# All attention matmuls on tiles of 64 rows by 32 columns, v's products by row halves into two banks

## The chip, the cores and the metric

The kernel runs on one core of one Trainium2 chip. The metric is device time in microseconds. The kernel before takes 1523.57 us, the median of three runs (1523.52 to 1525.18).

Engines by the names of the profile: PE is TensorE's matmul stream and PEld its weight loads, DVE is VectorE, ACT is ScalarE, POOL is GpSimd, SP is SyncE, which issues nearly all DMAs.

## The reference

A macaron transformer block on x of shape (2, 2048, 256), float32:

```
x = x + 0.5 * ffn(layernorm(x))
x = x + attention(layernorm(x))        # 16 heads of 16, softmax over 2048 keys, then @ wo.T + bo
x = x + 0.5 * ffn(layernorm(x))        # the same weights
ffn(h):  h = [h, -h] @ k0 (512 x 1024, entries +-1), * s0, relu, * 2
         h = h @ k1 (1024 x 1024), * s1, relu, * 2
         h = h @ k2 (1024 x 256), * s2
```

For each batch and head, scores are q k^T / 4, a softmax over the keys, and the product with v.

## The kernel before

**Blocks and layers.** The 4096 tokens go in 8 blocks of 512. For each block the feed-forward is three layers: l1 (8 output tiles of 128, inner dimension 256), l2 (8 tiles, inner 1024) and l3 (back to 256, tokens on partitions, 256 columns a matmul). Activations are held as two fp16 terms, a high and a low one, so each product is computed twice, with h_hi and with h_lo. A tile of l1 or l2 is emptied from PSUM in two operations: relu into the high term (ACT, L915, or DVE, L980), then relu minus the high term into the low one (DVE, L982). For q and k it is the same with L922 or L996, then L998. l3 is emptied by L987, v by L1006, the output projection by L1013, all on DVE.

**Attention.** A group is four heads of one block of 512 queries: 2 batches x 4 query blocks x 4 = 32 groups. The 2048 keys are 16 tiles of 128. An attention step (`Step("att", n)`) takes two key tiles of one group, so there are 8 steps a group and 256 in all. A step has 8 score banks of 128 keys by 512 queries: `pe_scores` (L856 to L874) computes them in four pairs of heads. Each matmul takes 64 rows (the four products of high and low terms of q and k, 16 dimensions each), so the two heads of a pair run on the upper and the lower 64 rows of the array, with 128 columns each. ACT takes the exponential of a bank, or of two neighbouring ones, into `prob` (`act_exps`, L942). `pe_values` (L876) multiplies the exponentials of the step before with v and a column of ones: 8 matmuls in fp32, 128 rows by 17 columns, the four heads of a key tile at partitions 0, 32, 64 and 96 of one bank (`O_BANK`). An fp32 matmul shows as two records. After 16 key tiles `dve_o` copies the bank out (L1115) and SP stores it. The division by the sum of the exponentials comes later (L1106, L1108).

**What is interleaved.** From attention's first step on, the other blocks' layers are cut into slots that are laid between the scores of the steps. `lay_pair` takes two banks of a layer at a time, always banks 6 and 7 (`SHARED`). In `pe_pair` (L798 to L854) one slot is two matmuls of 64 rows, one for each bank, on different row halves; after half of the slots the two banks change row halves, and PE waits for `halves` there (L816). At its first slot a pair waits until ACT and DVE have emptied both banks of the pair before (L802 to L806). The list `PAIRS` says how many slots a step holds and how they are divided by the scores; a step holds 8 slots of l1 or l2, 16 of l3, 2 of q and k, 4 of v or of the output projection. A pair of l1 banks has 8 slots (one step), of l2 32 (four steps), of l3 64 (four steps), of q and k 4, of v or the output 8 (two steps each). In a pair, the first bank of l1, l2, q and k is emptied wholly by DVE, the second by ACT (high) and DVE (low).

**Order.** The list `work`, written before the program, fixes the order on every engine; each engine walks it and takes its own parts, in order. A step of before is: scores of pairs 0 and 1; slots; score 2; slots; score 3; the values of the step before, both key tiles. Scores rotate over five banks (`SCORES`, 0 to 4), and a score waits (L864) for the exponential that read its bank last. Long DVE work (norms, splits, divisions) is laid behind a step's first scores (`lay_long`). In four steps the sum of squares of q and k (L775, 128 rows by 32 columns) takes one of the score banks (`lay_column`).

Before and after attention the layers are computed with matmuls of 128 rows by 128 columns (`pe_fill`, L738 for l1, L750 for l2, L762 for l3) in a ring of banks `WHOLE`, which is the score banks and the shared ones.

## Time and profile before

| | |
|---|---|
| runs | 1523.57 us median, 1523.52 to 1525.18 |
| profiled execution, span from first to last instruction | 1521.2 us |
| PE, PEld | 1512.4 us (99%), 606.1 us (40%) |
| ACT | 1129.3 us (74%) |
| DVE | 574.2 us (38%) |
| granted TensorE clock, mean | 0.999 |

The profile has no time of its own for the profiled execution beside its span; the span lies 2.4 us under the median of the runs.

A row of the time line has the start (us), the length (us, from the first start to the last end of the merged instructions), engine, line, operation, the tiles written and read, the shape and the count. A matmul's row lasts longer than the array is taken by it, since its filling and draining are in it: two matmuls that start 0.216 us apart each last 0.38. Times between starts are therefore what is to be read. In a matmul's shape `64*128` are the rows and columns of the array that its weights take, and `64x512` the moving data.

### The profile page before, as it was taken

Reading aid. Unit: us, or ns where it says so; the run is one execution under the profiler, and the core shown is the slowest. Engines: PE = TensorE matmul, PEld = TensorE weight load, DVE = VectorE, ACT = ScalarE, POOL = GpSimd, SP = SyncE. Lnnn points to the kernel's source line nnn. Section 1 sums busy time; section 2 is a strip of 40 time slices with the busy share of each in tenths; the row PEclk is TensorE's granted clock in tenths of the full one; section 3 lists DMA queues with packets and bytes.
Section 4 is the critical chain, followed back from the end, with each engine's and each line's share of the span. In section 5 each row is a group of like instructions: output and inputs, shape, how many; then the busy total and the mean of one; then the engine's idle time right before and its main releaser. Section 6 shows DMA issues by size and latency. Waiting matters only on the chain.

```text
span 1521.2 us, 31574 instructions
## 1 busy us (share of the span) xinstructions
PE 1512.4 (99%) x12471; PEld 606.1 (40%) x12471; DVE 574.2 (38%) x1298; ACT 1129.3 (74%) x1654; POOL 59.7 (4%) x65
## 2 busy tenths in 40 slices
PE   9999999999999999999999999999999999999999
PEld 5555455334334333333333334334333334334354
DVE  7645764511431243234332333242241332323462
ACT  3221222888889988898989989889988988988721
POOL 2010011001000100010100000000000000000000
PEclk9999999999999999999999999999999999999999
DMA  4122223212331231232223123111213212311110
GB/s 139 42 84 51 75 80 113 71 51 81 84 73 41 96 95 40 67 113 63 81 53 95 40 53 94 39 49 59 81 39 67 82 51 65 104 41 21 47 28 16
DMA packets 110139, 101.46 MB, mean 67 GB/s; under 512 B 55846, under 2 KB 95526, under 8 KB 109990
## 3 DMA queue, kind: packets, MB, share of 16 engines
q1 hardware_dynamic: 109158, 98.60, 23.0%
q8 instruction: 105, 1.72, 0.5%
q10 hardware_dynamic: 832, 0.79, 0.2%
q14 instruction: 44, 0.36, 0.1%
HBM read 61.87 MB, written 25.43 MB: 57 GB/s over the span
## 4 chain that ended last, share of the span: by engine, by line
PE 99%; DVE 0%; ACT 0%; issue 0%; POOL 0%; POOLq 0%
PE psum L888 31%; PE psum L850 30%; PE psum L872 16%; PE psum L750 12%; PE psum L762 3%; PE psum L738 3%; PE psum L769 2%; PE psum L782 1%; PE psum L688 0%; PE psum L775 0%; DVE xn L972 0%; DVE h_lo L982 0%; PE psum L710 0%; DVE x_sb L987 0%; ACT xn L911 0%
## 5 line engine op out<-in xcount | busy, mean ns | idle before, releaser
L942 ACT ACTIVATE prob<-psum 128x512 f32<-128x512 f32 (+1 forms) x1438 | 1016.6, 784 | 120.1 <-PE psum L872 115.4
L888 PE MATMUL psum<-prob,v_sb 128*17 128x512 f32 x4096 | 489.4, 595 | 0.0
L872 PE MATMUL psum<-q_st,k_st 64*128 64x512 f16 x2048 | 350.1, 379 | 0.2
L915 ACT ACTIVATE h_hi<-psum 128x512 f16<-128x512 f32 x183 | 109.6, 604 | 215.8 <-PE psum L750 164.6
L980 DVE TENSOR_SCALAR h_hi<-psum 128x512 f16<-128x512 f32 x73 | 50.5, 692 | 433.8 <-PE psum L850 433.8
L982 DVE SCALAR_TENSOR_TENSOR h_lo<-psum,h_hi 128x512 f16<-128x512 f32 x256 | 169.0, 688 | 86.9 <-ACT h_hi L915 84.4
L888 PEld LDWEIGHTS psum<-prob,v_sb 128*17 128x17 f32 x4096 | 95.3, 96 | 262.9 <-issue 166.4
L872 PEld LDWEIGHTS psum<-q_st,k_st 64*128 64x128 f16 x2048 | 82.5, 94 | 279.1 <-ACT prob L942 210.7
L850 PE MATMUL psum<-h_hi,w 64*128 64x512 f16 x1184 | 152.1, 376 | 0.2 <-ACT h_hi L915 0.2
L850 PE MATMUL psum<-h_lo,w 64*128 64x512 f16 x1184 | 152.0, 376 | 0.0
L750 PE MATMUL psum<-h_hi,w 128*128 128x512 f16 x432 | 102.5, 380 | 2.2 <-DVE h_lo L982 2.2
L750 PE MATMUL psum<-h_lo,w 128*128 128x512 f16 x432 | 103.4, 383 | 0.0
L850 PEld LDWEIGHTS psum<-h_hi,w 64*128 64x128 f16 x1184 | 58.0, 94 | 70.3 <-DVE h_lo L982 1.7
L850 PEld LDWEIGHTS psum<-h_lo,w 64*128 64x128 f16 x1184 | 57.8, 94 | 69.8
L1115 DVE COPY o_sb<-psum 128x512 f32<-128x512 f32 x32 | 22.1, 692 | 165.2 <-PE psum L888 164.8
L850 PE MATMUL psum<-xn,w 64*128 64x512 f16 x576 | 74.3, 377 | 0.0
L987 DVE SCALAR_TENSOR_TENSOR x_sb<-psum,scal,x_sb 128x512 f32<-128x512 f32 x32 | 23.2, 748 | 108.4 <-PE psum L850 77.4
L750 PEld LDWEIGHTS psum<-h_lo,w 128*128 128x128 f16 x432 | 42.7, 99 | 52.5 <-issue 2.2
L750 PEld LDWEIGHTS psum<-h_hi,w 128*128 128x128 f16 x432 | 42.2, 98 | 53.1 <-issue 2.7
L1106 DVE RECIPROCAL den_t<-den_t 128x128 f32<-128x128 f32 x64 | 60.5, 945 | 3.3 <-DMA den_t<-den_rows 3.3
L738 PE MATMUL psum<-xn,w 128*128 128x512 f16 x224 | 50.4, 379 | 1.1 <-ACT xn L911 0.9
L850 PE MATMUL psum<-w,h_lo 64*128 64x256 f16 x576 | 43.2, 269 | 0.0
(109 smaller groups left out, 860.0 us busy)
## 6 DMA issues: line engine op xcount, KB each, us to landing
k_st<-k_halves SPq DMA_DIRECT2D x64, 512.0 KB, 4.4
q_halves<-piece SPq DMA_DIRECT2D x32, 256.0 KB, 2.5
q_st<-q_halves SPq DMA_DIRECT2D x64, 128.0 KB, 4.8
x_rows<-x_sb SPq DMA_DIRECT2D x16, 256.0 KB, 2.2
k_halves<-piece SPq DMA_DIRECT2D x16, 256.0 KB, 2.8
att_rows<-o_sb SPq DMA_DIRECT2D x128, 32.0 KB
x_sb<-x_rows SPq DMA_DIRECT2D x8, 512.0 KB, 4.0
att_t<-att_rows SPq DMA_DIRECT2D x16, 256.0 KB
```

The lines of the kernel that those rows point to most:

```text
L738: mm = pe.matmul(psum[:, bank, :], w0[:, k, m * P:(m + 1) * P], xt[:, half, k, :], start=(j == 0), stop=(j == s.n - 1))
L750: mm = pe.matmul(psum[:, bank, :], w1[:, k, m * P:(m + 1) * P], (h0_hi, h0_lo)[half][:, k, :], start=(j == 0), stop=(j == s.n - 1))
L762: mm = pe.matmul(psum[:, bank, t * dim:(t + 1) * dim], (h1_hi, h1_lo)[half][:, k, tile * P:(tile + 1) * P], w2[:, k, :], start=(jj == 0), ...
L769: mm = pe.matmul(psum[:, bank, :], w[:, j, half * P:(half + 1) * P], at[:, j, :], start=(j == 0), stop=(j == kd - 1))
L850: mm = pe.matmul(to, w, a, start=(turned == 0 and j == 0), stop=(turned == 1 and j == length - 1))
L872: mm = pe.matmul(psum[:, score_bank[h + r], :], k_st[rows, slot, t * P:(t + 1) * P], q_st[rows, slot, :], start=True, stop=True)
L888: mm = pe.matmul(psum[32 * j:32 * j + va, O_BANK, :], v_sb[:, b * key_tiles + t, GROUP * g4 + j, :], prob[:, h % PROBS, :], start=(t == 0) ...
L915: act.activation(hi, psum[:, bank, :], ACT.Relu).then_inc(act_done, 1)
L942: act.activation(prob[:, to:to + count, :], psum[:, bank:bank + count, :], ACT.Exp, scale=score_scale / QK_SCALE ** 2).then_inc(exp_sem, 1)
L980: dve.tensor_scalar(hi[:, m, :], psum[:, bank, :], 0.0, None, ALU.max).then_inc(dve_done, 1)
L982: dve.scalar_tensor_tensor(lo[:, m, :], psum[:, bank, :], 0.0, hi[:, m, :], ALU.max, ALU.subtract).then_inc(dve_done, 1)
L1106: dve.reciprocal(den_t[:, half, cols], den_t[:, half, cols]).then_inc(den_inv, 1)
```

## The change

- Scores and all interleaved layers: each matmul of 64 rows by 128 columns becomes four of 64 rows by 32 columns (`QUARTERS`), each writing 32 partitions of the same bank.
- `pe_values`: each matmul of 128 rows by 17 columns becomes two of 64 rows by 17 columns, the upper keys into bank 4, the lower into bank 5 (`O_BANKS`). It is called once for each key tile, the two calls at different places in the step.
- `dve_o`: a copy of the one bank and then an addition of the other, with a wait between them.
- Four score banks instead of five; all exponentials are of two banks, but for one pair in a step with a column. A column takes two places in the rotation of the banks (`score_skip`).
- `WHOLE` has six banks instead of seven.
- The order of a step: score 0; slots; score 1; slots; the values of the first key tile of the step before; score 2; slots; score 3; the values of the second key tile. The slots of a step are as many as before, in three parts instead of two; for l1 and l2 2, 2 and 4.

```diff
@@ -121,8 +121,8 @@
-    SCORES = [0, 1, 2, 3, 4]
-    O_BANK = 5
+    SCORES = [0, 1, 2, 3]
+    O_BANKS = [4, 5]
     SHARED = [6, 7]
     def projections(u):
@@ -204,7 +204,7 @@
     ahead_of_attention = [s.kind in FILLS for s in side[:[(s.kind, s.u) for s in side].index(("l2", qblocks + 1))]]
-    in_turn = SCORES[:4] + SHARED + SCORES[4:]
+    in_turn = SCORES + SHARED
     WHOLE = [in_turn[(i - sum(ahead_of_attention)) % len(in_turn)] for i in range(len(in_turn))]
     numbers = Numbers()
@@ -227,7 +227,7 @@
-    PAIRS = {"l1": (4, 4), "l2": (5, 3), "l3": (10, 6), "qk": (1, 1), "v": (2, 2), "out": (2, 2)}
+    PAIRS = {"l1": (2, 2, 4), "l2": (2, 2, 4), "l3": (4, 4, 8), "qk": (0, 1, 1), "v": (1, 1, 2), "out": (1, 1, 2)}
     LONG = {"norm": 1.0, "xn": 0.3, "split": 0.4, "flip": 1.0, "merge": 0.4, "heads": 0.26, "peak": 0.3}
@@ -300,6 +300,10 @@
                 exp_groups.append((h, count))
                 exp_done.extend(count * (len(exp_groups),))
+    def score_skip():
+        taken.append(taken[-len(SCORES)])
     def lay_column(s):
         kind, h = taken[-len(SCORES)]
         assert kind == "exp"
@@ -307,6 +311,7 @@
         lay(s, SCORES[len(taken) % len(SCORES):][:1], False)
         taken.append(("dve", s.dve - 4 if s.kind == "range" else s.dve))
+        score_skip()
     for n in range(att_steps):
         work.append(Step("att", n))
@@ -318,25 +323,28 @@
         elif n >= 4 and side[0].hi + sum(PAIRS["l2"]) < 2 * FILLS["l2"][0]:
             lay_long(1.0)
-        for between, slots in enumerate(((5, 3), (3, 3), (3, 2), (3, 2))[n] if n < 4 else PAIRS[side[0].kind]):
-            lay_pair(slots)
+        for between, slots in enumerate(((2, 2, 4), (2, 2, 2), (1, 2, 2), (1, 2, 2))[n] if n < 4 else PAIRS[side[0].kind]):
+            if slots:
+                lay_pair(slots)
+            if between == 1 and n:
+                work.append(Step("values", n - 1, 0))
             work.append(Step("score", n, 1 + between))
         if n == 0:
             lay_pair(8)
         if columns and not side[0].n:
-            lay_exps(n, ((0, 1), (1, 2), (3, 1), (4, 1), (5, 2), (7, 1)))
+            lay_exps(n, ((0, 2), (2, 2), (4, 1), (5, 1), (6, 2)))
             lay_column(columns.pop(0))
         else:
-            lay_exps(n, ((0, 1), (1, 2), (3, 2), (5, 2), (7, 1)))
+            lay_exps(n, ((0, 2), (2, 2), (4, 2), (6, 2)))
         if n:
-            work.append(Step("values", n - 1))
+            work.append(Step("values", n - 1, 1))
             if n % group_steps == 0:
                 work.append(Step("o", n // group_steps - 1))
         if n == group_steps * (groups // 2 - 1):
             assert ("v", blocks - 1, 1) in find
-    work.append(Step("values", att_steps - 1))
+    work += [Step("values", att_steps - 1, tile) for tile in range(2)]
     work.append(Step("o", groups - 1))
     while held:
@@ -520,7 +528,7 @@
             sem(n) for n in ("ln", "ln_x", "split", "flipped", "merged", "squared", "peaked", "bo_added", "halves"))
         qk_sem, exp_sem, pv_sem = sem("qk"), sem("exp"), sem("pv")
-        o_copied, den_inv, att_ready = sem("o_copied"), sem("den_inv"), sem("att_ready")
+        o_half, o_copied, den_inv, att_ready = sem("o_half"), sem("o_copied"), sem("den_inv"), sem("att_ready")
         g_zero, g_in, g_pe, g_max, g_mout, g_mrow, g_exp, g_pv, g_o = (
             sem(n) for n in ("g_zero", "g_in", "g_pe", "g_max", "g_mout", "g_mrow", "g_exp", "g_pv", "g_o"))
@@ -666,10 +674,9 @@
                 if s.kind == "att":
                     pe_attention(s.u)
                 elif s.kind == "score":
-                    for pair in ((0, 1), (2,), (3,))[s.m]:
-                        pe_scores(s.u, pair)
+                    pe_scores(s.u, s.m)
                 elif s.kind == "values":
-                    pe_values(s.u)
+                    pe_values(s.u, s.m)
                 elif s.kind == "att_end":
                     pe.wait_ge(exp_sem, len(exp_groups))
@@ -795,6 +802,8 @@
             return 2 * tpb * out_no(u) + tpb + per_bank * (m + 1)
+        QUARTERS = [slice(c, c + P // 4) for c in range(0, P, P // 4)]
         def pe_pair(s):
             u, n = s.u, s.mate.n
@@ -835,7 +844,7 @@
                 for bank, first in ((s, 0), (s.mate, 1)):
                     r, m = (first + turned + part) % 2, bank.m
                     rows, cols = slice(64 * r, 64 * r + 64), slice(m * P, (m + 1) * P)
-                    to = psum[:, bank.bank, :]
+                    wide = slice(0, BANK)
                     if s.kind == "l1":
                         w, a = w0[rows, k, cols], xt[rows, term, k, :]
                     elif s.kind == "l2":
@@ -845,9 +854,11 @@
                     else:
                         tile = m * per_bank + column
                         src, wide_w = {"l3": ((h1_hi, h1_lo)[term], w2), "v": (at, wv_sb), "out": (att_t, wo_sb)}[s.kind]
-                        to = psum[:, bank.bank, column * dim:(column + 1) * dim]
+                        wide = slice(column * dim, (column + 1) * dim)
                         w, a = src[rows, k, tile * P:(tile + 1) * P], wide_w[rows, k, :]
-                    mm = pe.matmul(to, w, a, start=(turned == 0 and j == 0), stop=(turned == 1 and j == length - 1))
+                    for c in QUARTERS:
+                        mm = pe.matmul(psum[c, bank.bank, wide], w[:, c], a,
+                                       start=(turned == 0 and j == 0), stop=(turned == 1 and j == length - 1))
                     if i == 2 * n - 1:
                         mm.then_inc(mm_done, 1)
                     elif not turned and j == length - 1:
@@ -869,25 +880,28 @@
                     pe.wait_ge(dve_done, left[1])
             for r in range(2):
                 rows = slice(64 * r, 64 * r + 64)
-                mm = pe.matmul(psum[:, score_bank[h + r], :], k_st[rows, slot, t * P:(t + 1) * P], q_st[rows, slot, :],
-                               start=True, stop=True)
+                for c in QUARTERS:
+                    mm = pe.matmul(psum[c, score_bank[h + r], :], k_st[rows, slot, t * P:(t + 1) * P][:, c],
+                                   q_st[rows, slot, :], start=True, stop=True)
             mm.then_inc(qk_sem, 1)
-        def pe_values(n):
+        def pe_values(n, tile):
             g, tp = divmod(n, group_steps)
             b, g4 = g // (qblocks * block_groups), g % block_groups
-            for tile in range(2):
-                t = 2 * tp + tile
-                if t == 0:
-                    pe.wait_ge(o_copied, O_ZEROED + g)
-                    pe.wait_ge(dve_done, find["v", (b + 1) * qblocks - 1, 1].dve)
-                for j in range(GROUP):
-                    h = STEP_BANKS * n + GROUP * tile + j
-                    if j % 2 == 0:
-                        pe.wait_ge(exp_sem, exp_done[h + 1])
-                    mm = pe.matmul(psum[32 * j:32 * j + va, O_BANK, :], v_sb[:, b * key_tiles + t, GROUP * g4 + j, :],
-                                   prob[:, h % PROBS, :], start=(t == 0), stop=(t == key_tiles - 1))
-                mm.then_inc(pv_sem, 1)
+            t = 2 * tp + tile
+            if t == 0:
+                pe.wait_ge(o_copied, O_ZEROED + g)
+                pe.wait_ge(dve_done, find["v", (b + 1) * qblocks - 1, 1].dve)
+            for j in range(GROUP):
+                h = STEP_BANKS * n + GROUP * tile + j
+                if j % 2 == 0:
+                    pe.wait_ge(exp_sem, exp_done[h + 1])
+                for r in range(2):
+                    rows = slice(64 * r, 64 * r + 64)
+                    mm = pe.matmul(psum[32 * j:32 * j + va, O_BANKS[r], :],
+                                   v_sb[rows, b * key_tiles + t, GROUP * g4 + j, :], prob[rows, h % PROBS, :],
+                                   start=(t == 0), stop=(t == key_tiles - 1))
+            mm.then_inc(pv_sem, 1)
         def pe_attention(n):
             if n % group_steps == 0:
@@ -900,7 +914,7 @@
             for s in steps:
                 u, m, bank = s.u, s.m, s.bank
                 if s.kind == "score":
-                    act_exps(s.u, (0, 4, 6)[s.m], (4, 6, 8)[s.m])
+                    act_exps(s.u, 2 * s.m, 2 * s.m + 2)
                 elif s.kind == "w1":
                     act_w1()
                 elif not s.on_act or s.kind not in FILLS or not s.last():
@@ -1112,7 +1126,9 @@
             dve.wait_ge(pv_sem, key_tiles * (g + 1))
             if g >= 2:
                 dve.wait_ge(o_out[g % 2], O_MOVE * (g // 2))
-            dve.tensor_copy(o_sb[:, g % 2, :], psum[:, O_BANK, :]).then_inc(o_copied, 1)
+            dve.tensor_copy(o_sb[:, g % 2, :], psum[:, O_BANKS[0], :]).then_inc(o_half, 1)
+            dve.wait_ge(o_half, g + 1)
+            dve.tensor_tensor(o_sb[:, g % 2, :], psum[:, O_BANKS[1], :], o_sb[:, g % 2, :], ALU.add).then_inc(o_copied, 1)
         def dve_peak():
             dve.wait_ge(dve_done, find["sq", blocks - 1, 0].dve)
@@ -1376,7 +1392,7 @@
         sp_loads()
         act_loads()
         dve.memset(table[:], 1.0).then_inc(table_seed, 1)
-        dve.memset(psum[:, O_BANK, :], 0.0).then_inc(o_copied, 1)
+        dve.memset(psum[:, O_BANKS[0]:O_BANKS[1] + 1, :], 0.0).then_inc(o_copied, 1)
         act.wait_ge(table_seed, 1)
         act.activation(table[0:1, 0:1], table[0:1, 1:2], ACT.Exp).then_inc(table_ready, 1)
         act_factors()
```

## Rows read from the trace of the kernel before

**Rows 1.** Busy time of the engines, from the page.

```profile
PE 1512.4 (99%) x12471; PEld 606.1 (40%) x12471; DVE 574.2 (38%) x1298; ACT 1129.3 (74%) x1654; POOL 59.7 (4%) x65
```

**Rows 2.** The chain that ended last, shares by engine, from the page.

```profile
PE 99%; DVE 0%; ACT 0%; issue 0%; POOL 0%; POOLq 0%
```

**Rows 3.** Attention: length, then PE, PEld, DVE, ACT, POOL busy; clock, DMA share, GB/s.

```profile
278.18:1431.06 1152.88, 1152.70 (x10579) 415.15 (x10575) 370.10 (x781) 1033.85 (x1503) 35.15 (x24) 1.00 0.23 66
```

**Rows 4.** Time line of PE over one l2 step.

```profile
857.60 0.60 PE L872 MATMUL psum<-q_st,k_st 64*128 64x512 f16 x4
858.04 1.24 PE L850 MATMUL psum<-h_lo,w 64*128 64x512 f16 x10
...
859.99 0.38 PE L872 MATMUL psum<-q_st,k_st 64*128 64x512 f16 x2
860.30 1.91 PE L888 MATMUL psum<-prob,v_sb 128*17 128x512 f32 x16
862.14 0.60 PE L872 MATMUL psum<-q_st,k_st 64*128 64x512 f16 x4
```

**Rows 5.** Time lines of PE and DVE where a pair of q and k ends.

```profile
365.21 0.38 PE L872 MATMUL psum<-q_st,k_st 64*128 64x512 f16 x2
365.43 0.59 PE L850 MATMUL psum<-at,wk_sb 64*128 64x512 f32 x1
...
365.86 0.59 PE L850 MATMUL psum<-at,wk_sb 64*128 64x512 f32 x1
...
368.00 0.74 DVE L998 SCALAR_TENSOR_TENSOR piece<-psum,bk_sb,piece 128x512 f16<-128x512 f32 x1
```

**Rows 6.** Time line of PE in an l1 step, where the row halves change.

```profile
1409.48 0.38 PE L872 MATMUL psum<-q_st,k_st 64*128 64x512 f16 x2
1409.73 0.39 PE L850 MATMUL psum<-xn,w 64*128 64x512 f16 x2
```

**Rows 7.** Time lines of PE and DVE where a pair of l3 ends.

```profile
356.80 0.60 PE L850 MATMUL psum<-w,h_lo 64*128 64x256 f16 x8
...
357.43 1.41 DVE L987 SCALAR_TENSOR_TENSOR x_sb<-psum,scal,x_sb 128x512 f32<-128x512 f32 x2 [10.89 <-PE psum L850]
```

**Rows 8.** Time lines of DVE, PE and PEld where DVE was late.

```profile
286.30 0.69 DVE L982 SCALAR_TENSOR_TENSOR h_lo<-psum,h_hi 128x512 f16<-128x512 f32 x1 [0.42 <-ACT h_hi L915]
...
287.14 0.61 PE L850 MATMUL psum<-h_hi,w 64*128 64x512 f16 x4
...
287.11 0.14 PEld L850 LDWEIGHTS psum<-h_hi,w 64*128 64x128 f16 x4
```

**Rows 9.** A group by line and shape: count, busy us, mean ns, idle before.

```profile
L775 PEld LDWEIGHTS psum<-square,head_ones 128*32 128x32 bf16 x16 | 0.8, 92 | 3.4 <-issue 2.1 <-ACT h_hi L915 1.3
```

**Rows 10.** Time line of ACT, one narrow and two wide exponentials.

```profile
1408.60 2.43 ACT L942 ACTIVATE prob<-psum 128x512 f32<-128x512 f32 x3 [0.60 <-PE psum L872]
```

**Rows 11.** Time lines of PE and DVE where an l2 pair ends.

```profile
850.27 0.81 PE L850 MATMUL psum<-h_lo,w 64*128 64x512 f16 x6
...
853.51 0.59 PE L850 MATMUL psum<-h_hi,w 64*128 64x512 f16 x4
...
851.12 0.69 DVE L980 TENSOR_SCALAR h_hi<-psum 128x512 f16<-128x512 f32 x1 [16.07 <-PE psum L850]
851.84 1.29 DVE L982 SCALAR_TENSOR_TENSOR h_lo<-psum,h_hi 128x512 f16<-128x512 f32 x2
```

**Rows 12.** Line 982 in attention (count, ns min/median/max); time lines, output pair's end.

```profile
L982 DVE SCALAR_TENSOR_TENSOR h_lo<-psum,h_hi x144: 678/691/693, 285.2 to 1425.9; 128x512 f16<-128x512 f32 x144
...
776.98 0.81 PE L850 MATMUL psum<-wo_sb,att_t 64*128 64x256 f32 x6
777.90 1.29 DVE L1013 TENSOR_TENSOR x_sb<-psum,x_sb 128x512 f32<-128x512 f32 x2 [7.13 <-PE psum L850]
```

**Rows 13.** Time lines of PE and DVE where a group ends.

```profile
856.63 1.04 PE L888 MATMUL psum<-prob,v_sb 128*17 128x512 f32 x8
...
857.74 0.69 DVE L1115 COPY o_sb<-psum 128x512 f32<-128x512 f32 x1 [1.05 <-PE psum L888]
```

## The prediction

> **What bounds the kernel now.** I read the busy shares first: TensorE (PE) is busy for 99% of the span, ScalarE (ACT) for 74%, VectorE (DVE) for 38% [rows 1]. The chain that ended last says it in another way: 99% of it is PE [rows 2]. So what the change does to PE's order and waits is what it does to the time. The attention steps fill 278.18 to 1431.06 us, 253 whole steps and 76% of the span, with the granted clock at 1.00 (2.4 GHz) [rows 3]: 4.557 us a step.
>
> A PE row counts as busy from its start to a modelled end, so "99%" hides lost time; I find it from the starts. In one step [rows 4] scores start at 857.60, fills at 858.04, the last score at 859.99, v's products at 860.30 and the next scores at 862.14: 4.54 us. From 858.04 to 859.99 there are eight fill slots and a score, nine waves: a wave of 512 fp16 columns takes 0.216 us. Slots of q and k, in fp32, follow each other at 365.43 and 365.86 [rows 5]: a pass of 512 fp32 columns takes 0.43 us. A step holds 4 score waves, 8 fill waves and 4 passes: 12 x 0.216 + 4 x 0.43 = 4.31 us. The other 0.225 us lies where the tile shape changes: from the last score to the first product is 0.31 (0.09 too much), from the products to the next scores 1.84 instead of 1.72 (0.12); 0.01 is left. Between fills and scores, both 64x128, nothing is lost.
>
> **The change, part by part.**
>
> *One tile shape (64 rows by 32 columns).* The waves keep their number if the eight tiles run together: scores and fills 8 matmuls a wave instead of 2, v's products 8 on two row halves and four column groups, still 4 passes a step. Both changes of shape vanish. Of 256 steps I take off the two at the ends: gain 254 x 0.225 = 57.2 us; the bounds are 0 (the loss belongs to something else) and these 57. The four square steps keep their 128-row matmuls and so two changes: 0.9 us back. The wait between a pair's halves makes a wave of 0.25 us in an l1 step instead of 0.216, with the load behind it 0.05 in all [rows 6]; now products and scores lie there. With 36 l1 steps in attention (nine blocks of four pairs, a pair a step) that gives 1.8 us.
>
> *More instructions.* An l2 step has 128 matmuls and 128 loads instead of 40 and 40; an l3 step 192 and 192. The densest stream is that of l3: four slots (eight matmuls) last 0.60 us [rows 7], so with the slot of 0.109 us (four instructions) it is 27 ns each, and there the array was the limit, not the feed. The near end is a release from a wait: in program order loads and matmuls alternate, so the fourth load is the seventh instruction, and it starts 0.14 - 0.09 = 0.05 us after the first, 8 ns each [rows 8]. Needed are 16 per 216 ns (13 ns) in l2 and 16 per 109 ns (7 ns) in l3. At the far end an l2 step takes 256 x 0.027 = 6.9 us for 4.31, in all some +700 us. I take the near end, at no cost: it is the row with the array free. A load of 32 columns takes 92 ns [rows 9], less than the shortest slot, so loads hide.
>
> *Exponentials in pairs.* The eight banks of a step go as four wide ACT instructions. One narrow and two wide in a row take 2.43 us, so a wide one costs (2.43 - 0.61) / 2 = 0.91 [rows 10]. Four are 3.64, with a fill's relu 4.24 us: under 4.31, so ACT stays behind PE. I take 0; late by the relu once per l2 pair would be 36 x 0.5 = 18.
>
> *The place of the fills: a new wait.* This decides. DVE and ACT must empty a pair's banks (6 and 7) before the next pair may start. In an l2 pair of before the last slot starts at 850.27 + 2 x 0.216 = 850.70 and the next pair at 853.51, 2.81 later [rows 11]. DVE's three evacuations begin at 851.12 and end at 851.84 + 1.29 = 853.13 (the same group), 2.43 after the last slot. How long from there to PE's matmul shows where DVE was late: end 286.30 + 0.69 = 286.99, matmul 287.14, so 0.15 [rows 8]. Release is at 2.58, with 0.23 of slack today.
> The new order after the last slot is score, products of one key tile only (2 passes), score, fill: 0.216 + 0.216 + 0.86 + 0.216 = 1.51 us. So PE waits 2.58 - 1.51 = 1.07 us, with the second score (and its exponential) and the other products queued behind. By kind, with the pairs counted in the order of work (nine blocks' l1, l2 and l3, four blocks' q, k and v, seven blocks' output):
> - l1 and l2: 72 pairs (as the 144 h_lo say [rows 12]) x 1.07 = 77.0
> - l3: last slot 357.13, DVE ends 358.84 [rows 7], release at 1.86; order 0.109 + 1.292 = 1.40; 9 x 0.46 = 4.1
> - q and k: last slot 365.86, DVE ends 368.74 [rows 5], release at 3.03; order 0.43 + 1.292 = 1.72, or 1.94 ahead of another such pair; 4 x 1.31 + 4 x 1.09 = 9.6
> - output, and v taken the same: last slot 777.41, DVE ends 779.19 [rows 12], 1.93 against 1.51; 11 x 0.42 = 4.6
>
> Together 95.3 us for 100 pairs. From below, 0.04 instead of 0.15 for the release gives 84; from above, a long norm on DVE ahead of an evacuation adds some us.
>
> *The output of a group.* Two banks mean a copy (0.69) and an add (0.69, the same operation as the output's two in 1.29 [rows 12]), the add 0.72 after the copy's start as in the first two of [rows 11]: 1.41 us. DVE starts 0.07 after the products' end, 857.67 to 857.74 [rows 13], so 1.57 after the last slot; it ends at 2.98 and frees PE at 3.13. The next group's first product stands at 1.292 + 0.216 + 0.432 + 0.216 + 0.432 = 2.59: 0.54 us of wait. Where the step ended a pair (100 of 254), DVE begins at about 2.35 and PE is itself late: 3.91 against 2.59 + 1.07, 0.25. Mean 0.43 x 31 = 13.3 us. Bounds 0 (hidden, as the copy is now) and 20.
>
> *Outside attention* a ring of six banks replaces seven; a bank of l1 lasts four waves, 0.86 us, and is emptied within 2.6, so six are enough: 0.
>
> **Sum**, on the profiled execution: -57.2 + 0.9 - 1.8 + 95.3 + 13.3 = +50.5, a span of 1571.7 instead of 1521.2 us. The median of the runs, 1523.57, is 2.4 above that span, so 1574.
>
> **Rivals.**
> (a) *The feed falls behind in l3.* If an instruction takes half of the 27 ns of [rows 7], 13.6, an l2 step just fits and an l3 step takes 384 x 0.0136 = 5.22 instead of 4.33 us: 36 x 0.89 = 32 us, 1606. For it: no row shows a denser stream for more than seven instructions. Against it: those seven. The Trainium skill, "TensorE: Matmul & The Clock Gate", section "Wait — 56ns, not 53.3ns?", says that starts never come closer than about 25 ns however small the matmul; by that an l3 slot of eight would take 0.2 instead of 0.109 us, and my estimate from its figure is 36 x 16 x 0.091 = 52 us more. For different tiles the trace disagrees, with seven instructions in 0.05 us.
> (b) *The eight tiles do not run together* (row halves and column groups at once stand in no row, each alone does). Every fp16 wave doubled is 254 x 12 x 0.216 = 658 us, about 2235.
> (c) *The loss between shapes stays*, since it belongs to the turn from fp16 to fp32: 1574 + 57 = 1631. Against it: fp32 q and k follow fp16 scores at the usual distance, 365.21 to 365.43 [rows 5].
> (d) *The other side: the fill wait does not bind.* Its place is the first load after a step's first score. If PE let the second score and the products pass the waiting load, or the release came early, the gain would stand. It decides from 57.2 + 1.8 - 0.9 - 13.3 = 45 us over 100 pairs: 0.45 each instead of 0.95, for l1 and l2 a release 2.0 us after the last slot instead of 2.58. With no fill wait the time is 1574 - 95 = 1479. Against it: DVE ends 2.43 after the slot, and all of PE's instructions stand in one order.
>
> **Chances.** Forecast 0.73 (own range 1554 to 1590), (a) 0.12, (b) 0.03, (c) 0.05, (d) 0.07. The range 1552 to 1612 takes in the forecast with its bounds and (a). Under 0.2% (3 us) a measurement can't tell from none: faster 0.07, same 0.02, slower 0.91.
>
> **What would show it.** Right: no gap above a wave between scores and products; an l2 step in which no pair starts near 4.31 us, an l1 step near 5.4; a new pair's first matmul 0.15 us after DVE's last evacuation; more ACT idle time, put down to scores. Wrong: fill waves above 0.22 or 0.11 us (a, b), still 0.3 us from score to product (c), a pair's first matmul 1.5 us after the last slot (d).

## The result, and the profile after

The kernel with the change takes 1677.45 us, median of 4 runs (1670.65 to 1681.11), against 1523.57: 1.0998 times as long, with an interval of 1.0982 to 1.1013. The forecast was 1574, its range ended at 1612. The direction was right and the size was not: +154 us instead of +50.

The page of the kernel after: span, busy time [rows 1], the queue that brings instructions, and the chain [rows 2].

```profile
span 1676.2 us, 78723 instructions
PE 1522.6 (91%) x36439; PEld 806.7 (48%) x36439; DVE 593.9 (35%) x1330; ACT 1140.3 (68%) x1245; POOL 59.7 (4%) x65
q8 instruction: 292, 4.78, 1.2%
PE 80%; DVE 10%; issue 8%; ACT 2%; DMA 0%; ACTq 0%; DVEq 0%
```

PE has fallen from 99% to 91%, and the chain that was PE alone now holds DVE (the wait for a pair's banks, forecast) and 8% "issue", time in which PE waited for nothing that the profile shows. The instruction queue q8 brought 292 pages of 16 KB; before it had been:

```profile
q8 instruction: 105, 1.72, 0.5%
```

What ended PE's idle time in the kernel after (us in total, times, longest):

```profile
PE psum L860 <- DVE h_lo L996: 59.5, 64, 1.3
PE psum L860 <- issue: 41.9, 38, 4.4
PE psum L901 <- issue: 13.0, 12, 3.3
PE psum L884 <- issue: 10.8, 10, 2.4
```

Where nothing disturbs it, the new step is what the prediction made of it. PE's time line of the kernel after over one l2 step, which answers to [rows 4]:

```profile
869.81 0.43 PE L884 MATMUL psum<-q_st,k_st 64*32 64x512 f16 x8
870.02 0.64 PE L860 MATMUL psum<-h_lo,w 64*32 64x512 f16 x16
...
873.04 0.43 PE L884 MATMUL psum<-q_st,k_st 64*32 64x512 f16 x8
873.26 1.07 PE L901 MATMUL psum<-prob,v_sb 64*17 64x512 f32 x16
874.12 0.43 PE L884 MATMUL psum<-q_st,k_st 64*32 64x512 f16 x8
```

A wave of eight matmuls takes 0.216 us, score to products is a wave (873.04 to 873.26) and no longer 0.31, and the step from 869.81 to 874.12 takes 4.31 us. So the eight tiles do run together. At 521.02 it goes otherwise, in an l3 step:

```profile
521.02 0.78 PE L860 MATMUL psum<-w,h_lo 64*32 64x256 f16 x36
526.18 1.04 PE L860 MATMUL psum<-w,h_lo 64*32 64x256 f16 x28 [4.38 <-issue]
526.80 0.84 PE L884 MATMUL psum<-q_st,k_st 64*32 64x512 f16 x8
527.23 2.12 PE L901 MATMUL psum<-prob,v_sb 64*17 64x512 f32 x16
```

PE stops in the middle of a run of matmuls of one kind, between two that nobody else's work separates, for 4.38 us, and the waves behind it take 0.43 us instead of 0.216 until 530. The windows of the kernel after show why these waves are slow (length, PE, PEld, DVE, ACT, POOL busy, clock, DMA share, GB/s): the granted clock fell from 1.00 (2.4 GHz) to 0.50 (1.2 GHz) during the stall and stayed there when PE was busy again.

```profile
516.00:520.80 4.80, 4.41 (x200) 3.06 (x186) 0.00 (x0) 4.02 (x4) 0.00 (x0) 1.00 0.44 107
521.60:525.80 4.20, 0.20 (x14) 0.00 (x0) 0.00 (x0) 0.79 (x1) 0.00 (x0) 0.76 0.58 181
523.90:530.50 6.60, 4.32 (x100) 2.91 (x107) 0.99 (x2) 1.67 (x2) 0.00 (x0) 0.50 0.04 13
```

By kind of step, worked out from the trace as distances between the attention steps (255 of them, each from the start of the last matmul of a step's first pair of scores to that of the next step; sums in us). The last row is the experiment e10, explained below:

| | l2 (145) | l3 (36) | q, k (16) | v (8) | l1 (36) | output (14) | all |
|---|---|---|---|---|---|---|---|
| before | 657.3 | 164.1 | 72.9 | 36.8 | 166.8 | 64.1 | 1162.0 |
| after | 702.8 | 224.2 | 78.6 | 43.6 | 198.2 | 72.5 | 1319.9 |
| after, median step | 4.34 | 5.75 | 4.67 | 5.72 | 5.42 | 5.45 | |
| the tenth experiment | 667.1 | 170.7 | 79.9 | 39.4 | 188.4 | 71.2 | 1216.7 |

The sum grows by 158 us and the span by 155; outside attention 3 us were gained. The largest part is l3, the densest in instructions: 384 of PE a step, against 256 in l2.

### The profile page after: what moved, and what is told of

It reads as the page before. It is cut to its first block, busy times and chain, and to the rows that moved or that the text cites. A ratio compares the mean times of both kernels' runs of the same rounds, so it can differ in the third digit from the quotient of the medians.

```text
span 1676.2 us, 78723 instructions
## 1 busy us (share of the span) xinstructions
PE 1522.6 (91%) x36439; PEld 806.7 (48%) x36439; DVE 593.9 (35%) x1330; ACT 1140.3 (68%) x1245; POOL 59.7 (4%) x65
## 4 chain that ended last, share of the span: by engine, by line
PE 80%; DVE 10%; issue 8%; ACT 2%; DMA 0%; ACTq 0%; DVEq 0%
PE psum L860 27%; PE psum L901 22%; PE psum L757 11%; PE psum L884 11%; DVE h_lo L996 4%; PE psum L769 3%; DVE h_hi L994 3%; PE psum L745 3%; PE psum L776 2%; ACT prob L956 1%; PE psum L789 1%; DVE o_sb L1129 1%; DVE o_sb L1131 1%; DVE x_sb L1001 1%; DVE v_sb L1020 0%
## 5 line engine op out<-in xcount | busy, mean ns | idle before, releaser
L956 ACT ACTIVATE prob<-psum 128x1024 f32<-128x1024 f32 x1029 | 1024.0, 1020 | 265.8 <-PE psum L884 248.7
L901 PE MATMUL psum<-prob,v_sb 64*17 64x512 f32 x8192 | 590.8, 593 | 17.2 <-issue 13.0
L884 PE MATMUL psum<-q_st,k_st 64*32 64x512 f16 x8192 | 492.2, 379 | 18.3 <-issue 10.8
L884 PEld LDWEIGHTS psum<-q_st,k_st 64*32 64x32 f16 x8192 | 168.2, 92 | 220.0 <-ACT prob L956 114.6
L901 PEld LDWEIGHTS psum<-prob,v_sb 64*17 64x17 f32 x8192 | 159.2, 94 | 115.9 <-issue 45.6
L860 PE MATMUL psum<-h_hi,w 64*32 64x512 f16 x4736 | 182.8, 377 | 29.5 <-DVE h_lo L996 25.8
L996 DVE SCALAR_TENSOR_TENSOR h_lo<-psum,h_hi 128x512 f16<-128x512 f32 x256 | 168.1, 686 | 83.8 <-ACT h_hi L929 81.3
L860 PE MATMUL psum<-h_lo,w 64*32 64x512 f16 x4736 | 186.3, 379 | 7.7 <-issue 7.7
L860 PEld LDWEIGHTS psum<-h_hi,w 64*32 64x32 f16 x4736 | 85.3, 92 | 110.3 <-DVE h_lo L996 42.5
L860 PEld LDWEIGHTS psum<-h_lo,w 64*32 64x32 f16 x4736 | 91.4, 93 | 75.4 <-issue 44.5
L860 PE MATMUL psum<-xn,w 64*32 64x512 f16 x2304 | 87.6, 377 | 23.6 <-DVE h_lo L996 18.9
L860 PEld LDWEIGHTS psum<-xn,w 64*32 64x32 f16 x2304 | 36.8, 92 | 71.4 <-DVE h_lo L996 33.2
L757 PEld LDWEIGHTS psum<-h_hi,w 128*128 128x128 f16 x432 | 42.2, 98 | 51.2 <-issue 0.6
L757 PEld LDWEIGHTS psum<-h_lo,w 128*128 128x128 f16 x432 | 42.2, 98 | 51.0
```

The costliest lines, as they stand in the source:

```text
L757: mm = pe.matmul(psum[:, bank, :], w1[:, k, m * P:(m + 1) * P], (h0_hi, h0_lo)[half][:, k, :], start=(j == 0), stop=(j == s.n - 1))
L860: mm = pe.matmul(psum[c, bank.bank, wide], w[:, c], a, start=(turned == 0 and j == 0), stop=(turned == 1 and j == length - 1))
L884: mm = pe.matmul(psum[c, score_bank[h + r], :], k_st[rows, slot, t * P:(t + 1) * P][:, c], q_st[rows, slot, :], start=True, stop=True)
L901: mm = pe.matmul(psum[32 * j:32 * j + va, O_BANKS[r], :], v_sb[rows, b * key_tiles + t, GROUP * g4 + j, :], prob[rows, h % PROBS, :], star ...
L956: act.activation(prob[:, to:to + count, :], psum[:, bank:bank + count, :], ACT.Exp, scale=score_scale / QK_SCALE ** 2).then_inc(exp_sem, 1)
L996: dve.scalar_tensor_tensor(lo[:, m, :], psum[:, bank, :], 0.0, hi[:, m, :], ALU.max, ALU.subtract).then_inc(dve_done, 1)
```

## The experiments

Ratios are to the kernel before, with 95% intervals. The theory: PE's instructions come in pages of 256 (16 KB), and the pages come too slowly. Rivals: the order (the fill wait larger than forecast), the eight tiles themselves, or the four score banks.

**e1: the order of before, two tiles a wave.** The four banks and the halved products stay. Of the edit, the lists and the tiles are shown; the lines that lay both key tiles' products at the step's end and two score pairs at its start are left out here.

```
-    PAIRS = {"l1": (2, 2, 4), "l2": (2, 2, 4), "l3": (4, 4, 8), ...}
+    PAIRS = {"l1": (4, 4), "l2": (5, 3), "l3": (10, 6), ...}
-                    for c in QUARTERS:
+                    for c in [slice(0, P)]:
```

> v's products by row halves (64x17) into two banks and four score banks, but the order of before (both key tiles at the step's end, slots 5 and 3) and scores and fills on 64x128 tiles. It has 4096 matmuls more than before, not 23968. If the loss at the change of shape hangs on the rows alone (128 to 64), it is gone here and nothing else is added: a step of 4.31 us, about 1467 to 1475 us. If it hangs on the columns too (128 to 32), the 0.3 us from score to product stay: about 1523. The theory that instruction fetch makes the part of the loss that I had not forecast expects no page stall here, since a step has 96 instructions; the theory that eight tiles at once are slow expects the products to take more than 0.43 us a pass.

Measured 1576.3 us, 1.0342 [1.0325, 1.0359]. Both expected times were missed: the four score banks and the halved products in the old order cost 53 us by themselves. PE's time line over one l2 step:

```profile
869.02 0.61 PE L881 MATMUL psum<-q_st,k_st 64*128 64x512 f16 x4
869.46 1.24 PE L857 MATMUL psum<-h_lo,w 64*128 64x512 f16 x10
870.62 0.39 PE L881 MATMUL psum<-q_st,k_st 64*128 64x512 f16 x2
870.83 0.82 PE L857 MATMUL psum<-h_lo,w 64*128 64x512 f16 x6
871.53 0.39 PE L881 MATMUL psum<-q_st,k_st 64*128 64x512 f16 x2
871.86 1.94 PE L898 MATMUL psum<-prob,v_sb 64*17 64x512 f32 x32
873.73 0.61 PE L881 MATMUL psum<-q_st,k_st 64*128 64x512 f16 x4
```

The step takes 4.71 us, 0.40 above twelve waves and four passes. Score to products is 0.33 (0.11 too much) and products to scores 1.87 (0.15), although both now use 64 rows: 128 columns against 17 are enough for the loss between shapes. Five fill waves take 1.16 instead of 1.08 and three 0.70 instead of 0.65: both times the score behind them waits for the exponential that frees its bank.

**e2: the new order, two tiles a wave** (only the second edit of e1).

> The changed kernel with its order, but scores and fills on 64x128 tiles again (2 matmuls a wave, not 8): the instructions of the change are taken away, its waits are not. Fetch theory: no stall longer than the fill wait, and the time is that of e1 plus the forecast's two waits, 95 and 13 us: about 1575 if e1 is near 1467 (1630 if e1 is near 1523, and more since products now stand at two places of a step). Rival, the order alone makes all of the loss: within 1% of the changed kernel, 1677.

Measured 1671.51, 1.0965 [1.0947, 1.0984], with no idle time of PE put down to issue and 137 pages. The condition set for the rival (within 1% of the change) is met, yet the rival isn't shown by it, for this is another sum: an l2 step is 4.816 us (median), 0.51 above 4.307, with four changes of shape in it, and PE has none of the 65.7 us that it loses to issue in the change. The likeness of the totals is luck. Together e1 and the forecast's two waits would be 1685.

**e3: the old order, eight tiles** (only the first edit of e1).

> The changed kernel with all its 64x32 tiles, in the order of before: the waits are taken away, the instructions are not. Fetch theory: 1467 plus the 100 us that the forecast did not have, about 1570, with gaps of 1 to 4 us on PE that end about 1.3 us after a page of instructions has landed. Rival (the order alone): 1467 to 1480, with no such gaps.

Measured 1677.17, 1.1023 [1.1005, 1.1041]: the order of before doesn't save the eight tiles. Its waits:

```profile
PE psum L857 <- issue: 44.7, 37, 5.1
PE psum L881 <- issue: 29.9, 20, 4.5
PE psum L898 <- issue: 16.1, 17, 3.1
```

The fill wait is gone and the loss by issue has grown to 90.7 us; a median l2 step takes 4.496, an l3 step 6.24. The time is 107 us above the 1570 expected, mostly because that was built on 1467 for e1.

**e4: the new order, only the fills on 64 x 128.**

> The changed kernel with only the fills back on 64x128 tiles; scores stay on 64x32. An l2 step has 160 instructions instead of 256, an l3 step the same instead of 384. Fetch theory: the page stalls go, about the time of e2. If going between 64x128 and 64x32 costs what a change of shape cost before (0.1 us), six changes more in a step are 254 x 0.6 = 150 us more than e2.

Measured 1727.24, 1.1332 [1.1313, 1.1351]: the slowest. It is 56 us above e2, not 150: a step has six changes of shape against e2's four, not six more. They make the l2 step 5.02 us, 0.71 above 4.307. PE's time line in it:

```profile
850.14 0.40 PE L884 MATMUL psum<-q_st,k_st 64*32 64x512 f16 x8
850.47 0.61 PE L860 MATMUL psum<-h_hi,w 64*128 64x512 f16 x4
851.01 0.41 PE L884 MATMUL psum<-q_st,k_st 64*32 64x512 f16 x8
...
854.08 0.41 PE L884 MATMUL psum<-q_st,k_st 64*32 64x512 f16 x8
854.30 1.04 PE L901 MATMUL psum<-prob,v_sb 64*17 64x512 f32 x16
```

Score to fill takes 0.33 (0.12 too much), fill to score 0.54 for two waves of 0.43 (0.11); from 32 to 17 columns, 854.08 to 854.30, nothing is lost.

**e5: a probe.** Ahead of the kernel before, PE runs waves of matmuls on ready data with no waits. From 25.6 us on nothing else runs; the kernel's own loads, still under way, fall into the first stretch. One execution only, read by its trace.

```
+ for size, n, waves in ((32, 512, 64), (32, 256, 128), (32, 128, 96),
+                        (128, 256, 64), (128, 128, 128), (128, 64, 128)):
+   each wave: 2 row halves x 128/size column tiles, n columns moved
```

> The kernel before with a stretch of fp16 matmuls put in front of it, back to back with no waits: eight tiles of 64x32 with 512 columns (64 waves), 256 (128 waves), 128 (96 waves), then two tiles of 64x128 with 256, 128 and 64 columns. It measures the feed by itself. Fetch theory: 512 columns, 16 instructions a wave, a page of 256 in 16 waves of 0.216 = 3.5 us, just about sustained (0.216 to 0.24 us a wave); 256 columns is limited by pages, 0.22 to 0.24 us a wave instead of 0.109; 128 columns the same 0.22 to 0.24. In the two-tile stretches a wave of 4 instructions can't be below 0.055 to 0.06, so 256 and 128 columns take 0.109 and 0.06, and 64 columns 0.055 to 0.06 instead of 0.03. Rival (dispatch as fast as the 8 ns of the release row, pages no limit): 0.216, 0.128, 0.128 and 0.109, 0.055, 0.032.

The time line of PE in the second stretch, eight tiles with 256 columns (the first row begins in the stretch of 512 and runs into it):

```profile
25.19 3.82 PE L704 MATMUL psum<-ident 64*32 64x512 f16 x216
30.29 1.94 PE L704 MATMUL psum<-ident 64*32 64x256 f16 x128 [1.28 <-issue]
33.74 1.94 PE L704 MATMUL psum<-ident 64*32 64x256 f16 x128 [1.51 <-issue]
```

This is the cause by itself. PE runs exactly 128 matmuls and 128 loads, 256 instructions, and stops; the next 256 begin 3.45 us after the last 256 began. That is the shortest round: over the twelve rounds from 30.29 to 75.57 it is 3.45 to 4.00 us, 3.77 on average (14.7 ns an instruction). Set against the transfers of q8, a round has three parts: the next page's transfer starts 1.04 to 1.15 us after PE has begun a page, takes 0.9 to 1.5, and PE begins that page 1.35 to 1.59 us after its end. The rounds differ by the transfer's length. The DMA view of 25 to 42 us shows what comes meanwhile, 16 KB at a time, with all other queues silent (packets, MB, share):

```profile
DMA packets 4, 0.07 MB, mean 4 GB/s; under 512 B 0, under 2 KB 0, under 8 KB 0
q8 instruction: 4, 0.07, 1.6%
```

Within a page the stream is quick: 128 waves of eight took 28.52 us in all, but the median wave took 0.109, 16 instructions at 7 ns each. Two tiles of 128 columns run without a stop, and their 128 waves are 512 instructions in 7.07 us, 13.8 ns each, about the quickest rate of the pages. The first, second and fifth stretch in the window view:

```profile
5.35:25.60 20.25, 15.74 (x512) 7.85 (x519) 4.00 (x20) 0.00 (x0) 0.00 (x0) 0.93 0.63 186
25.64:54.16 28.52, 16.87 (x1032) 15.12 (x1024) 0.00 (x0) 0.00 (x0) 0.00 (x0) 0.92 0.02 5
...
85.53:92.60 7.07, 7.07 (x258) 7.07 (x254) 0.00 (x0) 0.00 (x0) 0.00 (x0) 1.00 0.02 5
```

Eight tiles with 256 and with 128 columns took 0.223 and 0.229 us a wave, as expected, the second at a clock of 0.50. Two tiles with 256 columns took 0.141, not 0.109, at a mean clock of 0.76. Two tiles with 64 columns took 0.045, below the expected 0.055 to 0.06: 512 instructions in 5.82 us is more than pages bring, so a part of them must have been there already. The first stretch, eight tiles with 512 columns, took 0.316, above the expected 0.216 to 0.24. Here the DMA engines were 63% busy; one page's transfer began 7.2 us after the one before (13.52 to 20.73, from the transfers of q8 in the trace), and PE stood still for 3.37 us behind it:

```profile
23.10 5.90 PE L704 MATMUL psum<-ident 64*32 64x512 f16 x256 [3.37 <-issue]
```

The kernel after shows the same. I set PE's 60 idle times by issue against the transfers of q8: every one ends 1.19 to 1.59 us after the transfer of a page has ended. Of their 65.7 us, 42.2 (24 times) stand behind a page whose transfer began more than 6 us after that of the page before. Such late pages are 41 of the 272 in attention, and they go with DMA traffic: in the 3 us ahead of the late transfer the DMA engines were over 40% busy in 37 of the 41 cases, but only in 23 of the 158 where pages came up to 4.6 us apart. The stall at 521 is one of them. PE began the page before it at 518.95, and the next transfer started 4.84 us later, at 523.8, as the traffic ended; after PE's restart at 526.18 it took 1.26 us until the next one started. The DMA view of 520 to 527 us, busy tenths in 40 slices:

```profile
DMA  6996456329698577899989541000000000000000
```

**e6, e7 and e8: fewer instructions, the same waves.** In e6 (new order) and e7 (old order) the interleaved fills of l1, l2 and l3 run their first column tile alone, in e8 (new order) only those of l3 do; three quarters of these outputs are left out. A fill wave then has one tile on each row half and lasts as long. (Other tiles are free meanwhile, and six of a score's eight matmuls start ahead of a fill slot that stands before them in the program: e10, 850.13 against 850.22. An l2 step stays bound by the full tiles, 4.307 us.)

```
-                    for c in QUARTERS:
+                    for c in QUARTERS[:1 if s.kind in ('l1', 'l2', 'l3') else 4]:
```

> The changed kernel, but of each interleaved matmul of l1, l2 and l3 only the first of the four column tiles is issued: three quarters of these layers' output columns are left out. Tiles, order, waits, waves and all other engines' work stay; a step has 160 instructions instead of 256 (l3: 384). Fetch theory: the gaps that are no wait for an engine go, and what stays is what the forecast had, 1574 us (1566 to 1582). Rival (the part of the loss that was not forecast comes from the waits being longer than sized, or from eight tiles at once): above 1650.

> As the run before it, in the order of before (64x32 tiles throughout, three quarters of the interleaved l1, l2 and l3 columns left out). It is e1 without its two changes of tile shape a step. If a change costs what it did before, 254 x 0.215 = 55 us less than e1: 1522. Were the shape worth nothing: 1576. Fetch theory: no page stalls, against e3's 1677.

> The changed kernel, with three quarters of the columns left out in l3's interleaved matmuls alone (36 of 256 steps). Fetch theory: the l3 steps fall from 6.2 us to 4.3 and 4.5 us, 65 us in all, and some of the stalls of the l2 steps behind them go as well: 1585 to 1612. If the loss is spread by instruction count over all steps: 1650.

Measured: e6 1584.55, 1.0402 [1.0384, 1.042]; e7 1555.71, 1.021 [1.0193, 1.0227]; e8 1624.26, 1.0664 [1.0643, 1.0685]. e6 is 3 us above the expected range, and its largest wait is the one that the prediction had, 65.1 us for L996; 3.9 us go to issue. e7 lies between its two expected values and still has 14.2 us of idle time by issue. e8 lies 12 us above its range and far below the 1650 of its rival.

So 92.9 us of the time after hang on the number of instructions, 53.2 of them on l3 alone; e8's l2 steps still sum to 700.5 us, so l2 has stalls of its own and doesn't merely pay off the debt of l3.

**e9: a complete kernel meant to beat both.** Eight tiles except in steps with l3 fills, the old order, l2 slots (6, 2), one wait for a pair of scores.

```
+                for c in ([slice(0, P)] if n in dense else QUARTERS):
```

> A try at a version that beats both: 64x32 tiles in all steps but those with l3 slots, where scores and fills stay on 64x128; the order of before, with slots 6 and 2 in l2; one wait instead of two ahead of a pair of scores whose banks one ACT instruction frees. Complete, nothing left out. An l2 step should take 4.33 us plus what is left of page stalls (0 to 0.3), an l3 step 4.6 (two changes of shape), l1 4.5: 1505 us if pages keep up at 256 instructions in 4.33 us, 1545 if l2 steps lose 0.3 us each as in e3.

Measured 1539.72, 1.0098 [1.0081, 1.0115]: it beats the change, not the kernel before, and is near the worse of its two expected times. A median l2 step is 4.407 against 4.537, but the mean 4.563 against 4.533: 19.7 us of idle time by issue (9.6 + 8.3 + 1.8) eat it.

**e10 and e11: e6 and e7 with v and the output cut as well** (their kinds added to the list; three quarters of these outputs too are left out). **e12: e11 with one wait**, for the later of the two exponentials of a pair of score banks, in place of one for each bank.

```
+            both = bank_left[h:h + 2]
+            if all(kind == "exp" for kind, _ in both):
+                pe.wait_ge(exp_sem, max(exp_done[left] for _, left in both))
+                both = []
```

> e6 (the changed kernel with three quarters of the interleaved l1, l2 and l3 columns left out) with the same done for v and the output projection, the steps that still had 256 instructions in e6. Fetch theory: the last of the page stalls go, 10 us less than e6's 1585, and the forecast's 1574 stands (1570 to 1578). Rival (what is left in e6 is something else in these steps): 1585 as before.

> The same in the order of before. e7 came out at 1556, 34 us above the 1522 worked out from e1; its output and v steps, with 256 instructions, were 1.0 and 0.8 us longer than the rest. Fetch theory: 1522 to 1530. Rival (one shape is worth 20 us only): 1550 to 1556.

> e11 with one wait instead of two ahead of a pair of scores whose banks one ACT instruction frees. In e1, e3 and e7 the third pair of scores starts 0.14 us after its exponential has ended, and a step of l2 is 0.18 us over its 4.31 us. If 0.1 of that is the second wait, which PE takes as an instruction of its own, an l2 step falls from 4.49 to 4.39 us and the time by 20 to 26 us; if the exponential itself is late, by less than 5 us.

Measured: e10 1578.0, 1.0356 [1.0339, 1.0374], a span of 1573.3; e11 1535.45, 1.0075 [1.0059, 1.0092]; e12 1504.14, 0.9868 [0.9852, 0.9885]. e10 lies at the upper end of its range; e11 is 5 us above its own and far below its rival. The waits of PE in e10:

```profile
PE psum L860 <- DVE h_lo L996: 64.1, 68, 1.3
PE psum L901 <- DVE o_sb L1131: 8.1, 26, 0.3
```

e10 is close to the kernel that the prediction described, whose additional instructions cost next to nothing (1.4 us by issue): 1578 against the forecast 1574, span 1573.3 against 1571.7. The change is 99.5 us above it. In the old order the instructions cost more, e3 less e11, 141.7 us. In e12 the second wait alone was worth 31.3 us, more than the 20 to 26 expected (3.8 of it is idle time by issue, which e12 doesn't have), and the median l2 step fell from 4.493 to 4.407. e6, e7, e8, e10, e11 and e12 leave outputs out, so e12's time is not that of a usable kernel.

## Why the prediction was right and wrong

- *One tile shape, -57.2 us (0.225 a step): right.* With the order and banks the same, the l2 step of e1 (two tiles) is 4.706 and that of e11 (one shape) 4.493: 0.213, times 254 is 54 us. The runs differ by 40.9 only; e11 waits 7.7 us more for exponentials and 3.8 us for issue. Not foreseen: a change of columns alone, at 64 rows, costs as much, about 0.12 us each (median l2 steps of 4.307, 4.816 and 5.02 us with none, four and six of them).
- *More instructions, "I take the near end, at no cost": this step failed.* It cost 99.5 us (after less e10). The near end was a burst of seven instructions at 8 ns, and that was true, even for 256 at 7 ns; it was a rate of dispatch. What binds is how fast pages arrive, which no burst shorter than a page can show: 3.45 to 4.00 us a page in e5, 13.5 to 15.6 ns an instruction. The count of pages stood in the profile (105), and was not read: 292 of them in 1676 us are one per 5.7 us on average, but one per 4.31 in an l2 step and 1.5 per l3 step.
- *Rival (a)* had the right rate by luck, as half of a figure that the array had set: 13.6 ns an instruction is 3.48 us a page, and e5 has 3.45 at best, 3.77 on average. It priced l3 alone and at an even flow: 5.22 us a step, 32 us in all. l3 steps took 5.75 (median) and 6.23 (mean), 53.5 us above e10, and the others, which it let go free, 35.7 (l2), 9.8 (l1) and 4.2 (v). A median l3 step is what 1.5 pages take at 3.77 us each, 5.66. An l2 step needs one page in 4.31 us, so it has little to spare, and a page that is late by more is a stall; these late pages are what rival (a) did not have. Of the 99.5 us, 65.7 are idle time of PE by issue (41.9 + 13.0 + 10.8). The clock is a part of the rest: in five stretches of the kernel after, behind 315, 445, 523, 694 and 1022 us, it was 0.50, for 20 us in all with PE busy in 18 of them, which costs at most 9 us; in e10 it never fell before the end. I haven't divided the rest further.
- *The page's rule.* That starts never come closer than about 25 ns however small the matmul (the Trainium skill, "TensorE: Matmul & The Clock Gate", section "Wait — 56ns, not 53.3ns?") doesn't hold across tiles: e5 has eight matmuls in 0.109 us, 14 ns each. The estimate from it, +52 us for l3, lies close to the measured 53.5 for another reason.
- *The fill wait, +95.3 us: right in kind, a little high.* Time lines of PE and DVE in the kernel after where a pair ends, here one of l1 (the prediction read an l2 pair, [rows 11]):

```profile
407.65 1.06 PE L860 MATMUL psum<-xn,w 64*32 64x512 f16 x32
...
409.59 0.41 PE L884 MATMUL psum<-q_st,k_st 64*32 64x512 f16 x8
410.92 0.62 PE L860 MATMUL psum<-xn,w 64*32 64x512 f16 x16 [0.92 <-DVE h_lo L996]
...
408.76 0.69 DVE L994 TENSOR_SCALAR h_hi<-psum 128x512 f16<-128x512 f32 x1 [3.36 <-PE psum L860]
409.49 1.29 DVE L996 SCALAR_TENSOR_TENSOR h_lo<-psum,h_hi 128x512 f16<-128x512 f32 x2
```

  The last slot starts at 407.65 + 3 x 0.216 = 408.30, DVE ends at 409.49 + 1.29 = 410.78, and PE's first matmul comes 0.14 later, 2.62 after the slot (forecast 2.58), where the order had it at 1.51: 1.11 instead of 1.07. The profile calls only 0.92 of it idle, since the matmul before counts as busy to its modelled end. Over e10, from the starts, 67 waits behind l1 and l2 pairs cost 1.10 each, and all 87 ahead of fills 85.6 us. Rival (d) fell.
- *The output of a group, +13.3 us: right.* e10 has 26 such waits with 8.1 us of idle time; from the starts each is late by 0.47, 12.3 us in all. *ACT, 0: nearly right* for the new order, whose undisturbed step is 4.31, with 11 waits for exponentials and 4.5 us of idle time in e10. In the old order it would have been wrong: four banks make PE wait for exponentials (e1), 0.18 us a step in e11 (4.493 against 4.31), half of which goes when the pair's two waits become one (e12, 4.407).
- *Squares and the halves of l1*, +0.9 and -1.8, are below what the runs separate. The nearness of e10 to the forecast is in part luck: the fill term was 10 us too high, and waits that the sum had at nothing make up for it. *Rivals (b) and (c)* fell: waves of 0.216 us, 0.22 from score to products.

Still open: whether the DMA traffic is what makes pages late (they go together in the kernel after and in e5's first stretch, but no run changed the traffic alone), why the transfer of an undisturbed page takes 0.9 us at one time and 1.5 at another, and how what the clock leaves of the remaining 34 of the 99.5 us divides.

## What to carry to other kernels

Count instructions per microsecond for each stage before cutting matmuls into smaller tiles: here 256 of PE's instructions came per 3.45 us at best and 3.77 on average, so a stage that asks for more than one page per some 4 us stalls, however full the array is, and one that asks for a page per 4.31 us stalls whenever a page is late. A burst in a trace gives the rate of dispatch and not that of supply; for supply read the instruction queue's pages against the time of the stage. The profile's idle time of PE leaves out a part of each wait, so take what a wait costs from the starts. With few buffers, price the slowest chain of waits between a producer and its next turn, and let one wait stand for two.

## What the runs showed of the hardware

- PE's instructions arrive 16 KB, 256 instructions, at a time. While PE waits for them, pages come 3.45 to 4.00 us apart in the silent probe; in the attention of the kernel after no two are closer than 3.3 us, and 41 of 272 are over 6. A starved PE shows as idle time by issue in mid-stream, up to 5.1 us of it at once (e3), and in the kernel after it always starts again 1.19 to 1.59 us after a page's transfer has ended.
- The clock fell to 0.50 (1.2 GHz) during the long stall, at about 523.8 us, and was 0.50 until 530.5, while PE was busy again from 526.18 on.
- Eight tiles of 64 x 32 run at once: 0.216 us for 8 matmuls of 512 columns, 0.109 for 256.
- A change of tile shape costs about 0.12 us, for 128 to 32 or 17 columns too, but nothing from 32 to 17.
- Matmuls on different column tiles don't always start in the program's order: in e10 six matmuls of a score start at 850.13, ahead of a fill slot at 850.22 that stands before them.
- Two waits ahead of a matmul in place of one cost 0.09 us in the median l2 step, 31.3 us over e11, where the data is just late.
